# Logits of the second attention: full-array matmuls for pairs of heads, from queries stacked by VectorE

## What is computed

```
qp = q @ Wq.T                                   # [b, 256 tokens, 256]
scores = qp @ kv.T                              # kv: the context, 77 tokens
idx = argmax(scores, axis=-1)                   # one context token per query token
mem = kv[idx]                                   # 256 picked rows, with repeats
mk, mv = split(mem @ Wkv.T)                     # one key and one value of 16 numbers per row, shared by all heads
qh = qp split into 16 heads of 16
logits = qh @ mk.T / sqrt(16)                   # per head
attn = softmax(logits); out = attn @ mv
return out @ Wc.T
```

## Time and profile before

| | value |
|---|---|
| time, median of 3 runs | 1814.24 us (1812.26 to 1815.61) |
| the profiled execution, first to last instruction | 1871.9 us |
| PE busy | 1702.8 us, 91% |
| DVE busy | 1322.4 us, 71% |
| ACT busy | 985.6 us, 53% |
| POOL busy | 945.8 us, 51% |
| chain that ended last, by engine | PE 45%, issue 17%, DVE 14%, POOL 8%, DMA 8%, ACT 7% |
| PE, logits of the second attention (L1143) | 1024 matmuls of 308 columns in 512 pairs, 154.6 us busy |

### The profile page before, as it was taken

How to read it: one execution, slowest core, us unless ns; L and a number is a source line. 1 busy time by engine, 2 the same in 40 slices (tenths; PEclk the granted TensorE clock), 3 DMA queues, 4 the chain that set the end, 5 groups by cost and what they waited for, 6 DMA issues and landing times.

```text
span 1871.9 us, 51471 instructions
## 1 busy us (share of the span) xinstructions
PE 1702.8 (91%) x17308; PEld 1435.5 (77%) x17308; DVE 1322.4 (71%) x4639; ACT 985.6 (53%) x2819; POOL 945.8 (51%) x1507
## 2 busy tenths in 40 slices
PE   3799999999999999999999999999999997448785
PEld 2688888888888888888888888888888876347675
DVE  5467777777777777777777777777777775436554
ACT  2355555555555555555555555555555554224443
POOL 2114555555555555555555555555555554345555
PEclk8899999999999999999999999999999999579998
DMA  7401111111000001000000000000000012138886
GB/s 219 145 9 50 44 40 38 41 41 35 25 24 22 31 14 31 30 21 24 23 25 24 27 19 20 20 22 17 23 23 20 21 45 73 47 91 209 193 199 138
DMA packets 102656, 101.12 MB, mean 54 GB/s; under 512 B 38879, under 2 KB 92073, under 8 KB 102616
## 3 DMA queue, kind: packets, MB, share of 16 engines
q1 hardware_dynamic: 68824, 81.43, 14.0%
q0 software_dynamic: 33792, 19.17, 5.9%
HBM read 51.63 MB, written 111.84 MB: 87 GB/s over the span
## 4 chain that ended last, share of the span: by engine, by line
PE 45%; issue 17%; DVE 14%; POOL 8%; DMA 8%; ACT 7%; SPq 1%; POOLq 0%; DVEq 0%; ACTq 0%
PE bank L1085 13%; PE bank L990 8%; DMA out<-ey,aid 7%; POOL table L615 5%; PE ps_lg L1143 3%; ACT p L802 3%; PE ps_yo L1099 3%; PE ps_yo L990 3%; PE bank L1071 3%; PE ps_tr L1016 3%; PE ps_m L990 2%; PE ps_pt L1158 2%; ACT xr L741 2%; DVE pt_l L1634 2%; DVE rmax L1629 2%
## 5 line engine op out<-in xcount | busy, mean ns | idle before, releaser
L615 POOL DMA_INDIRECT table<-xs,slot x496 | 504.0, 1016 | 201.5 <-issue 171.9
L802 ACT ACTIVATE p<-ps_lg,rmax 128x77 f32<-128x77 f32 x1024 | 235.6, 349 | 144.5 <-DVE rmax L1629 139.4
L1085 PE MATMUL bank<-h_h,held 128*128 128x256 f16 x2048 | 266.8, 273 | 4.1 <-issue 2.0
L557 POOL TENSOR_TENSOR pool_pad<-pad_in 128x1 f32<-128x1 f32 x352 | 67.9, 193 | 397.1 <-PE ps_lg L1143 176.8
L1085 PE MATMUL bank<-h_l,held 128*128 128x256 f16 x2048 | 266.8, 274 | 0.0
L1085 PEld LDWEIGHTS bank<-h_l,held 128*128 128x128 f16 x2048 | 201.0, 98 | 24.4 <-issue 0.6
L1085 PEld LDWEIGHTS bank<-h_h,held 128*128 128x128 f16 x2048 | 195.6, 98 | 28.4 <-DVE h_l L1564 2.6
L631 POOL TENSOR_TENSOR rs<-nt,minushalf 128x2 f32<-128x2 f32 x128 | 92.9, 726 | 200.2 <-DVE nt L1529 188.7
L1564 DVE SCALAR_TENSOR_TENSOR h_l<-bank,h_h 128x512 f16<-128x512 f32 x256 | 175.0, 684 | 11.6 <-ACT h_h L783 6.9
L1629 DVE TENSOR_REDUCE rmax<-ps_lg 128x8 f32<-128x616 f32 x128 | 101.8, 795 | 85.7 <-PE ps_lg L1143 84.7
L706 POOL DMA_INDIRECT out<-ey,aid x64 | 98.7, 1542 | 99.0 <-DVE aid L1902 65.0
(11 more groups left out here) (277 smaller groups left out, 4604.0 us busy)
## 6 DMA issues: line engine op xcount, KB each, us to landing
ew<-in_e_wts SPq DMA_DIRECT2D x48, 384.0 KB
table<-xg SPq DMA_DIRECT2D x8, 1284.0 KB, 16.0
xg<-table SPq DMA_DIRECT2D x64, 160.5 KB
xs<-xr SPq DMA_DIRECT2D x31, 320.0 KB, 2.6
x<-in_x SPq DMA_DIRECT2D x32, 256.0 KB
out<-x SPq DMA_DIRECT2D x32, 256.0 KB
table<-xs,slot POOLq DMA_INDIRECT x496
held<-in_e_wts SPq DMA_DIRECT2D x16, 384.0 KB, 4.4
```

The lines of the kernel that those rows point to most:

```text
L615: g.indirect_dma_start(out=table, out_offset=bass.IndirectOffsetOnAxis(ap=slots[:, t, k:k + 1], axis=0), in_=rows[:, t, :], in_offset=None ...
L802: ins = a.activation(p32[:, h * S2:(h + 1) * S2], ps_lg[:, h // HB, h % HB * S2:(h % HB + 1) * S2], ACT.Exp, bias=rmax[r % 2][:, h:h + 1])
L1085: ins = mm(two(bank[j % 2])[:, m % 2, :], wb1[:, k, m * P:(m + 1) * P], hp[:, k, :], start=(i == 0 and k == 0), stop=(i == 1 and k == FK - 1))
```

## The change

Three things change in the second attention.

- **The logits' matmuls.** A round has 4 matmuls instead of 8. Each uses all 128 rows of the array, has 154 columns (2 heads by 77 keys), and makes the logits of one pair of heads at once. The 128 rows are four quarters of 32: the pair's high queries, its low queries, its high queries again, and a constant 61440. Against them stand in `kst`: high keys, high keys, low keys, and the mask, which is 0 or -61440.
- **The stacks.** POOL makes the keys' part of `kst` with one instruction on 96 partitions instead of two of 308 columns on 128 (and one more small multiplication ahead of it). DVE writes the mask's quarter in `c_counts`, on 32 partitions and 154 columns. DVE also copies the queries' halves into `qst`, a new function `c_stack`: 12 copies per batch, each of 32 partitions by 512 fp16 numbers, from one quarter of the partitions to another. The constant quarter of `qst` is set once, at the start of DVE's program.
- **The order.** PE does `b_l1(0)` ahead of `c_lg(0)`, no longer behind it. DVE does `b_l0(3)` ahead of `c_counts`, and `c_stack` right behind it. `c_lg(0)` has one more wait, for `c_stack` (`qst_ok`).

The diff, cut to its core:

```diff
+PH = 2
+HP = HC // PH
+Q4 = P // 4
...
-NEG = -1e30
+FAR = 61440.0
...
+        kst = sb("kst", [P, PH, S2], F16)
+        qst = sb("qst", [P, C2, HP, S], F16)
...
                 g.tensor_copy(kr_h[:, :], kr32[:, :]).then_inc(kr_hi, 1)
                 pool.wait_ge(kr_hi, 2 * b + 2)
-                g.tensor_tensor(kr_l[:, :], kr32[:, :], kr_h[:, :], ALU.subtract).then_inc(handoff, 1)
-                hm = halfmask[:, :].unsqueeze(2).to_broadcast([P, HB, S2])
+                g.tensor_tensor(kr_m[:, :], kr_h[:, :], lowpart[:, 0:1].to_broadcast([P, S2]), ALU.mult).then_inc(kb_ok, 1)
+                pool.wait_ge(kb_ok, 3 * b + 1)
+                g.tensor_tensor(kr_x[:, :], kr32[:, :], kr_m[:, :], ALU.subtract).then_inc(handoff, 1)
                 pool.wait_ge(handoff, b + 1)
-                g.tensor_tensor(kb_h[:, :, :], kr_h[:, :].unsqueeze(1).to_broadcast([P, HB, S2]), hm, ALU.mult).then_inc(kb_ok, 1)
-                g.tensor_tensor(kb_l[:, :, :], kr_l[:, :].unsqueeze(1).to_broadcast([P, HB, S2]), hm, ALU.mult).then_inc(kb_ok, 1)
+                n = 3 * Q4
+                g.tensor_tensor(kst[0:n, :, :], kr_x[0:n, :].unsqueeze(1).to_broadcast([n, PH, S2]),
+                                pairmask[0:n, :].unsqueeze(2).to_broadcast([n, PH, S2]), ALU.mult).then_inc(kb_ok, 2)
...
-                    pe.wait_ge(kb_ok, 2 * b + 2)
+                    pe.wait_ge(kb_ok, 3 * b + 3)
                     pe.wait_ge(mrow_ok, b + 1)
+                    pe.wait_ge(qst_ok, b + 1)
                 else:
                     pe.wait_ge(p_ok.sem, p_ok.nth(r - 1, b))
                 tt = slice(t * P, (t + 1) * P)
 
-                for i, (keys, queries) in enumerate([(mrow, None), (kb_h, qp_h), (kb_l, qp_h), (kb_h, qp_l)]):
-                    for g_ in range(2):
-                        rows = slice(g_ * 64, (g_ + 1) * 64)
-                        ins = mm(ps_lg[:, g_, 0:HB * S2], row0[rows, :] if queries is None else queries[rows, c, tt], keys[rows, :, :],
-                                 start=(i == 0), stop=(i == 3))
+                for p in range(HP):
+                    g_, at = divmod(p, HP // 2)
+                    ins = mm(ps_lg[:, g_, at * PH * S2:(at + 1) * PH * S2], qst[:, c, p, tt], kst[:, :, :], start=True, stop=True)
                 ins.then_inc(lg_rdy.sem, 1)
...
+                if on(n):
+                    b_l1(0, n)
                 if on(c):
                     c_lg(0, c)
                     c_vb(c)
                 if on(n):
-                    b_l1(0, n)
                     b_l1(1, n)
...
+            def c_stack(b):
+
+                dve.wait_ge(qp_lo, b + 1)
+                for p in range(HP):
+                    mine = slice(p * Q4, (p + 1) * Q4)
+                    v.tensor_copy(qst[Q4:2 * Q4, :, p, :], qp_l[mine, :, :])
+                    v.tensor_copy(qst[0:Q4, :, p, :], qp_h[mine, :, :])
+                    last = v.tensor_copy(qst[2 * Q4:3 * Q4, :, p, :], qp_h[mine, :, :])
+                last.then_inc(qst_ok, 1)
...
                 dve.wait_ge(cnt_rdy, b + 1)
-                v.tensor_scalar(mrow[:, :, :], ps_tr[:, 2 * P:2 * P + S2].unsqueeze(1).to_broadcast([P, HB, S2]),
-                                0.0, NEG, ALU.is_equal, ALU.mult).then_inc(mrow_ok, 1)
+                far = slice(3 * Q4, P)
+                v.tensor_scalar(kst[far, :, :], ps_tr[far, 2 * P:2 * P + S2].unsqueeze(1).to_broadcast([Q4, PH, S2]),
+                                0.0, -FAR, ALU.is_equal, ALU.mult).then_inc(mrow_ok, 1)
...
                 if on(n):
                     b_l0(2, n)
+                if on(n):
+                    b_l0(3, n)
                 if on(c):
                     c_counts(c)
-                if on(n):
-                    b_l0(3, n)
+                    c_stack(c)
                 if on(d):
                     d_x4(d)
...
+            v.memset(qst[3 * Q4:P, :, :, :], FAR)
             ln_first(0)
```

More of the change, by code:

```diff
@@ L131, in build @@
         before16 = sb("before16", [P, P], F16)
-        row0 = sb("row0", [P, P], BF16)
         iota_k = sb("iota_k", [P, S2])
@@ L137, in build @@
         halfmask = sb("halfmask", [P, HB])
+        pairmask = sb("pairmask", [P, PH])
         pad_in = sb("pad_in", [P, 1])
@@ L208, in build @@
         cx_h, cx_l = sb("cx_h", [P, C2, S2], F16), sb("cx_l", [P, C2, S2], F16)
-        kr_h, kr_l = sb("kr_h", [P, S2], F16), sb("kr_l", [P, S2], F16)
-        kb_h, kb_l = sb("kb_h", [P, HB, S2], F16), sb("kb_l", [P, HB, S2], F16)
+        kr_h, kr_m, kr_x = (sb(name, [P, S2], F16) for name in ("kr_h", "kr_m", "kr_x"))
+        lowpart = sb("lowpart", [P, 1], F16)
+        kst = sb("kst", [P, PH, S2], F16)
+        qst = sb("qst", [P, C2, HP, S], F16)
         vpc = sb("vpc", [S2, DH])
@@ L216, in build @@
         hot = sb("hot", [P, T2, S2], F16)
-        mrow = sb("mrow", [P, HB, S2], BF16)
         cnt = sb("cnt", [S2, 1])
@@ L295, in build @@
         lt_ok, sg_ok = sem("lt_ok"), sem("sg_ok")
-        cx_ok, kr_hi = sem("cx_ok"), sem("kr_hi")
+        cx_ok, kr_hi, qst_ok = sem("cx_ok"), sem("kr_hi"), sem("qst_ok")
         handoff, kb_ok, ctx_hi = sem("handoff"), sem("kb_ok"), sem("ctx_hi")
@@ L508, in _ @@
             g.memset(before16[:, :], 1.0).then_inc(consts2, 1)
-            g.memset(row0[:, :], 0.0).then_inc(consts2, 1)
             g.memset(headmask[:, :], 1.0).then_inc(consts2, 1)
             g.memset(wide[:, :], 0.0).then_inc(consts2, 1)
-            pool.wait_ge(consts2, 5)
+            pool.wait_ge(consts2, 4)
             g.affine_select(out=ident[:, :], in_=ident[:, :], compare_op=ALU.not_equal, fill=1.0,
@@ L517, in _ @@
                             base=0, pattern=[[1, P]], channel_multiplier=-1).then_inc(consts2, 1)
-            g.affine_select(out=row0[:, :], in_=row0[:, :], compare_op=ALU.not_equal, fill=1.0,
-                            base=0, pattern=[[0, P]], channel_multiplier=1).then_inc(consts2, 1)
             g.affine_select(out=headmask[:, :], in_=headmask[:, :], compare_op=ALU.is_ge, fill=0.0,
@@ L524, in _ @@
                             base=P, pattern=[[-1, 3 * P]], channel_multiplier=1).then_inc(consts2, 1)
-            pool.wait_ge(consts2, 10)
+            pool.wait_ge(consts2, 8)
             g.affine_select(out=headmask[:, :], in_=headmask[:, :], compare_op=ALU.is_gt, fill=0.0,
                             base=DH, pattern=[[DH, HC]], channel_multiplier=-1).then_inc(consts2, 1)
-            g.affine_select(out=row0[:, :], in_=row0[:, :], compare_op=ALU.not_equal, fill=1.0,
-                            base=-P // 2, pattern=[[0, P]], channel_multiplier=1).then_inc(consts2, 1)
-            pool.wait_ge(consts2, 12)
+            pool.wait_ge(consts2, 9)
             g.tensor_tensor(halfmask[:, :], headmask[:, 0:HB], headmask[:, HB:HC], ALU.add).then_inc(consts2, 1)
+            pool.wait_ge(consts2, 10)
+            g.tensor_tensor(pairmask[:, :], halfmask[:, 0:PH], halfmask[:, PH:HB], ALU.add).then_inc(consts2, 1)
             g.iota(iota_k[:, :], pattern=[[1, S2]], base=0, channel_multiplier=0,
@@ L550, in _ @@
             g.memset(p32[:, HC * S2:PC * P], 0.0).then_inc(consts2, 1)
+            g.memset(lowpart[:, :], 1.0).then_inc(consts2, 1)
+            pool.wait_ge(consts2, 29)
+            g.affine_select(out=lowpart[:, :], in_=lowpart[:, :], compare_op=ALU.is_ge, fill=0.0,
+                            base=-2 * Q4, pattern=[[0, 1]], channel_multiplier=1).then_inc(consts2, 1)
             g.memset(pool_pad[:, :], 0.0).then_inc(consts2, 1)
```

## The result

| | before | after |
|---|---|---|
| time, median of 4 runs each | 1813.78 us (1812.26 to 1815.61) | 1924.48 us (1922.88 to 1928.88) |
| ratio after to before | | 1.061, 95% interval 1.059 to 1.0629 |
| the profiled execution, first to last instruction | 1871.9 us | 1927.1 us |
| PE busy | 1702.8 us, 91% | 1669.1 us, 87% |
| DVE busy | 1322.4 us, 71% | 1434.5 us, 74% |

What follows compares the result with a forecast made beforehand. PE was taken as the bound, busy 1341.10 of 1365.00 us in the loop. 3.1 us per turn plus 0.45 for the clock, over 31 turns 110 us, plus some 2 us, put 1814 at 1926; range 1862 to 1968.

Steps and rivals of the forecast that it cites:

- The counts and the copies: On DVE, new counts take about 1.0 us plus 0.2, then twelve copies at 0.32 us each, 3.84 us.
- The two waits: PE waits 3.0 us ahead of round 0's logits and 1.2 us ahead of the first turning of exponentials.
- The logits: On PE, a round of four matmuls takes 0.37 us instead of 0.63, saving 0.26 in each of 4 rounds.
- half was said to: Of four shorter logit rounds, only rounds 1 and 3 give time back, 0.52 us per turn.
- The clock: After the 3.0 us wait PE may fall to 1.2 GHz: at worst 1.65 us per turn, counted as 0.45.
- the first wait: PE ahead of round 0's logits, held by the copies on DVE: logits start at 819.4, 3.0 us later.
- the second wait of 1.2 us: PE ahead of the first turning, ready at 822.0 while the chain of maximum and exponentials ends at 823.2.
- that cover: PE's 1.2 us to spare before the turning absorbs part of the slow clock's 1.65 us, leaving 0.45.
- the sum: Per turn of the loop 3.1 us of lateness plus 0.45 for the clock, 3.55 us; 31 turns make 110 us.
- PE late by 3.6 at the turning: PE turns round 0's exponentials at 823.2 instead of 819.59, 3.6 us late; 0.52 comes back, leaving 3.1.
- If the profiler's 3.2% lies evenly: If the profile's excess over the runs lies evenly on everything, the 112 us loss would be 108.

Runs made afterwards that it cites:

- e3: Changed kernel with all twelve copies on partitions 0 to 31, eight into idle tiles, stack left wrong: 1932.12 us, ratio 1.0316.
- e9: Changed kernel with `b_l1(1)`, too, ahead of the first logits on PE: 2009.99 us, ratio 1.069 to the kernel before.
- e1: Changed kernel without its twelve copies, stacked queries left zero, new order kept: 1874.24 us, ratio 1.0003 to the kernel before.
- e7: Changed kernel without its twelve copies and with the old order on PE and DVE, the matmuls alone: 1839.17 us, ratio 0.9885.
- e8: Changed kernel's matmuls in the old order, stack made by five SyncE DMAs through the chip's memory instead of DVE copies: 1850.78 us, ratio 0.9841.
- e4: Changed kernel unaltered, run again on another chip beside the kernel before (1861.43 us there): 1964.78 us, ratio 1.0552.
- e6: Changed kernel, copies kept, with PE's and DVE's lists in the order of the kernel before: 2000.1 us, ratio 1.0745.
- e2: Kernel before with the new order alone, `b_l1(0)` ahead of the first logits and `b_l0(3)` ahead of the counts: 1905.84 us, ratio 1.0179.
- e0: Kernel before, unchanged, run and profiled once more: 1873.5 us, ratio 0.9987, span of its profile 1881.1 us.
- e10: Changed kernel with six of its twelve copies, part of the stack left zero: 1912.84 us, ratio 1.0173 to the kernel before.
- e5: Changed kernel's matmuls in the old order, stack made by twelve SyncE DMAs instead of DVE copies: 1966.42 us, ratio 1.0563.

## Why the prediction was right, and where it was not

**The counts and the copies.** From the mask to the first copy it said 1.2 us; it is 1.28. The values times the counts no longer meet POOL's DMA, 0.22 us instead of 0.48. The mask on 32 partitions holds DVE for 0.36 us (849.73 to 850.09), where 0.22 was forecast. A copy was put at 0.32 and took 0.295; e3 bears out the reason given, the changing partitions.

**The two waits.** 3.0 and 1.2 us were forecast, 3.03 and 1.27 are there, and e9 shows the 3.74 us of the chain bare. That the copies and nothing else make the loss is shown by e1.

**The logits.** A round was put at 0.37 us and takes 0.26, so the saving is 0.37 per round where 0.26 was forecast. The line through 77 and 256 columns gave 0.068 for 154; four take 0.27 with start and end, so the 0.1 us added for these was wrong. Half of it comes back: e7 measures 0.72 us per turn (22.3/31) of 4 x 0.37 = 1.48, as half was said to. Of round 0's shorter logits nothing does: in e7 and e8, as in the kernel before, the turning comes 5.0 us behind the last matmul of `d_dn(1)`.

**The clock.** It does fall: in the first profile the granted clock went to 0.5 around the first wait in 22 of the loop's turns, and in the profile before nowhere between 106 and 1549 us. But the cost was too high at 0.45 per turn. With the fall the turning in e4 comes 3.85 us after the logits, without it 3.74: 0.11 us, since the slow piece fits into the second wait of 1.2 us nearly whole; the prediction had named that cover and counted too little of it. Whole turns say the same. In the first profile turns with a short fall take 50.30 and those without 50.14; in six turns the fall lasts 6 to 7 us, and they take 51.2 or more. That is some 0.3 per turn on average. In e4, turns with and without a fall both take 51.4. Where the slow stretch doesn't fit, as in e6 and e9, it costs more than a microsecond per turn.

**The order.** The prediction had it inside the sum (PE late by 3.6 at the turning) and not as a term. Right for this kernel, but the runs show its size: without the copies it costs 0.7 us per turn (e1 against e7, by the ratios) to 1.1 (e2 against the kernel before), with them it saves 35 us in all (e4 against e6).

**The sum.** 3.55 us per turn were forecast. By the runs, where both kernels were measured together, it is 110.7/31 = 3.57 at first and 103.35/31 = 3.33 on e4's chip. The traces give less: 51.45 - 48.3 = 3.2 for e4 against e0, and only 50.3 - 48.3 = 2.0 for the two first profiles. The turn in stretches shows where this comes from (PE's rows, middle values of 26 turns, us):

| stretch | before, first profile | e0 | e4 | changed, first profile |
|---|---|---|---|---|
| last matmul of `d_dn(1)` to the first turning | 5.02 | 5.00 | 8.55 | 8.88 |
| to the logits of round 2 | 4.04 | 4.03 | 3.57 | 3.59 |
| to the logits of round 3 | 3.96 | 3.97 | 4.52 | 3.81 |
| to the counts of the next turn | 33.95 | 33.92 | 33.42 | 32.51 |

PE is late at the turning by 3.55 us in e4 and 3.86 in the first profile, where 3.6 was forecast: the copies, the two waits and the path to the turning are as the prediction had them. What comes back behind that is not. In e4, 0.46 and 0.50 come back and 0.55 is lost between the logits of rounds 2 and 3, net 0.4 where 0.52 was forecast; the loss is a late release that the prediction had no term for (last section). The first profile has 1.4 us less in the last stretch, where the change makes only round 3 shorter by 0.37.

So the mechanism was right, and the nearness of 1926 to 1924.48 owes something to luck: the copies were 0.3 us per turn too dear, the clock 0.15 to 0.4 too dear, and the late release was missing. With e4's ratio, 1814 would have become 1914.

**The gap of the profile.** "If the profiler's 3.2% lies evenly" was the wrong question: e0 shows that it is not the profiler's. In every stretch of the table the first profile of the kernel before is like e0, whose runs took 1873.5, and not like an execution of 1814 us, of which there is no trace. The 9 us between their spans (1871.9 and 1881.1) match the difference in PE's wait for DVE's `pt_l`, 5 times and 6.4 us in the one, 18 times and 15.9 in the other. The changed kernel's first profile, whose runs took 1924, differs from e4 mainly in the last two stretches. One mark of the last stretch: ACT waits ahead of `xr` 27 times and 17.7 us in e0's loop, 26 times and 14.9 us in e4's, and 2 times and 3.1 us in the changed kernel's first profile. What makes it so isn't in the profiles. The forecast could live with it because it was a difference put onto the median of the runs.

## What to carry to other kernels

Look for an engine's unbroken stretch on the way to the bound engine's next input, and price every instruction that you put there at its distance to the next one, not at its length. When work must wait, leave the bound engine one piece of other work ahead of the wait and one behind it: the one ahead shortens the wait, the one behind takes up the slow clock that follows. A rearrangement across partitions that is small in bytes can go by memory, in as few DMAs as possible, where each issue costs more than its bytes.

## What the runs showed of the hardware that was not expected

- SyncE's issue of a DMA within SBUF (32 partitions, 64 pieces of 512 bytes) takes 0.64 us; of one of 128 KB from memory to 32 partitions, 0.43 us (1.28 for three); of 128 KB out from 128 partitions, 0.35 us. Two legs through memory (first issue 847.63, logits at 853.16 with no wait) were quicker than one within SBUF in twelve parts (862.29 to 871.32).
- A release from PE in round 2 comes late in some kernels. In e4 the logits start at 874.55, but DVE's maximum and ACT's high half start only at 876.31 and 876.36:

```profile
876.31 0.80 DVE L1646 TENSOR_REDUCE rmax<-ps_lg 128x8 f32<-128x616 f32 x1 [0.59 <-PE ps_lg L1149]
```

```profile
876.36 0.49 ACT L814 ACTIVATE pt_h<-ps_pt 128x384 f16<-128x384 f32 x1 [0.89 <-PE ps_yo L1163]
```

In a turn of the changed kernel's first profile the logits of round 2 start at 862.03, ACT's high half at 862.84 and the maximum at 863.13: 0.8 and 1.1 us later, where e4 has 1.8 for both. PE waits for the result 0.97 us in e4 and 0.30 there. This is not a matter of the chip alone: from the logits to the maximum it is 2.2 us in e1, 1.9 in e2 and e10 and 2.0 in e3, but 1.2 in e5 and e6, which ran on e4's chip, and 1.1 in e9. It is also where most of the order's cost without copies lies: from the logits of round 2 to those of round 3 PE takes 4.98 us in e1 and 4.14 in e7. The cause stays open.
- The same kernel took 1814, 1861, 1874 and 1879 us on the four occasions of this study, 3.6% apart, while the ratio of the changed kernel to it, measured on two of them, moved only from 1.061 to 1.055. The cause stays open.
